# Second expert stage: gates spread through DRAM, all products in tiles of 64 by 64, two banks of sums

## The reference, cut to what matters

```python
flat = _rmsnorm(x, ln2_w).reshape(-1, Cx)
probs = jax.nn.softmax(flat @ router_w.T, axis=-1)
tp, ti = jax.lax.top_k(probs, TOPK)
tp = tp / (jnp.sum(tp, axis=-1, keepdims=True) + 1e-09)
weights = jnp.sum(tp[..., None] * jax.nn.one_hot(ti, NE, dtype=flat.dtype), axis=1)
for e in range(NE):
    hh = jax.nn.silu(flat @ w1[e].T) * (flat @ w3[e].T)
    out = out + weights[:, e:e + 1] * (hh @ w2[e].T)
return x + out.reshape(Bx, Tx, Cx)
```

## Time and profile before

| | us |
|---|---|
| median of 3 runs | 2643.34 |
| lowest and highest | 2638.82 and 2643.75 |
| the profiled execution's own time | 2647.51 |
| its span in the trace | 2645.6 |
| the second expert stage in it, from the first transpose | 2283.96 to 2645.6 |

### The profile page before, as it was taken

One profiled execution on the slowest core, in us unless ns is written; L12 is line 12 of the kernel. 1 busy time (PEld: TensorE's weight loads), 2 busy tenths in 40 slices (PEclk: granted clock), 3 DMA queues, 4 the chain that ended last, 5 costly groups with the idle time before them and its releaser, 6 DMA issues.

```text
span 2645.6 us, 50217 instructions
## 1 busy us (share of the span) xinstructions
PE 2413.0 (91%) x17762; PEld 1076.1 (41%) x17762; DVE 1835.3 (69%) x4773; ACT 1414.1 (53%) x2468; POOL 424.6 (16%) x505
## 2 busy tenths in 40 slices
PE   8987779999999999998699998987799998799999
PEld 3326623333333333334344444565544444433333
DVE  4566679888888888882456656569676773366665
ACT  2116727777777777774254453427567665144343
POOL 2002200000000000004322322132000012310110
PEclk9996769999999999997699996656699998599999
DMA  2114511010111101023555551245522242500110
GB/s 93 24 30 130 198 49 38 26 38 26 36 28 29 35 26 38 26 54 81 140 134 138 133 156 39 59 117 181 195 65 65 66 103 58 122 17 17 33 25 12
DMA packets 247843, 190.43 MB, mean 72 GB/s; under 512 B 190299, under 2 KB 195580, under 8 KB 247340
## 3 DMA queue, kind: packets, MB, share of 16 engines
q1 hardware_dynamic: 234426, 158.95, 22.4%
q0 software_dynamic: 10368, 19.06, 2.5%
q10 hardware_dynamic: 2808, 9.22, 1.5%
HBM read 121.58 MB, written 65.63 MB: 71 GB/s over the span
## 4 chain that ended last, share of the span: by engine, by line
PE 77%; DVE 8%; ACT 4%; DMA 3%; issue 3%; POOL 2%; SPq 1%; DVEq 0%; ACTq 0%; POOLq 0%
PE ps L1580 10%; PE ps L1486 7%; PE ps L1551 6%; PE ps L2785 4%; PE ps L2797 4%; PE ps L2291 4%; PE ps L2773 4%; PE ps L2306 4%; PE ps L1191 3%; PE ps L1165 3%; PE ps L364 3%; PE ps L1576 2%; PE ps L376 2%; PE ps L1103 2%; DMA mo_gate<-wg_d 1%
## 5 line engine op out<-in xcount | busy, mean ns | idle before, releaser
L1666 DVE TENSOR_REDUCE att_mpart<-ps 128x1 f32<-128x512 f32 x1024 | 633.5, 682 | 55.7 <-PE ps L1486 50.6
L1624 ACT ACTIVATE att_p<-ps 128x704 f32<-128x704 f32 x768 | 546.7, 761 | 214.8 <-PE ps L1551 207.6
L1580 PE MATMUL ps<-att_p,att_v 128*9 128x352 f32 x3072 | 300.7, 462 | 0.1
L1486 PE MATMUL ps<-att_kT,att_qT 64*128 64x512 bf16 x1024 | 281.0, 386 | 21.0 <-DMA att_qz<-qt_d 8.4
L1551 PE MATMUL ps<-att_qT,att_kT 64*128 64x352 bf16 x1536 | 251.4, 317 | 7.3 <-ACT att_p L1624 6.9
L1280 DVE TENSOR_REDUCE cau_mpart<-ps 128x1 f32<-128x512 f32 (+5 forms) x384 | 193.0, 551 | 81.2 <-PE ps L1106 61.1
L1247 ACT ACTIVATE cau_p<-ps 128x704 f32<-128x704 f32 (+6 forms) x272 | 171.5, 661 | 82.4 <-PE ps L1165 49.8
L2365 ACT ACTIVATE mo_g<-ps 128x768 f32<-128x768 f32 x176 | 133.3, 809 | 139.6 <-PE ps L2291 139.6
L2859 ACT ACTIVATE mo_act<-ps 128x1024 f32<-128x1024 f32 (+1 forms) x108 | 102.8, 952 | 196.3 <-PE ps L2773 196.1
L1457 POOL DMA_DIRECT2D o_d<-att_o x128 | 64.1, 507 | 841.1 <-ACT att_o L1607 840.9
L1551 PEld LDWEIGHTS ps<-att_qT,att_kT 64*128 64x128 bf16 x1536 | 82.0, 93 | 273.0 <-issue 263.3
(11 more groups left out here) (417 smaller groups left out, 3933.0 us busy)
## 6 DMA issues: line engine op xcount, KB each, us to landing
mo_gate<-wg_d SPq DMA_DIRECT2D x176, 192.0 KB, 4.2
qt_d<-pre_qT SPq DMA_DIRECT2D x8, 1056.0 KB, 4.3
kt_d<-pre_kT SPq DMA_DIRECT2D x8, 1056.0 KB, 7.0
att_kT<-kt_d SPq DMA_DIRECT2D x32, 264.0 KB, 2.7
att_qT<-qt_d SPq DMA_DIRECT2D x32, 264.0 KB, 3.0
cqt_d<-cpr_qT SPq DMA_DIRECT2D x8, 1056.0 KB
cau_qT<-cqt_d SPq DMA_DIRECT2D x16, 528.0 KB, 4.1
o_d<-att_o POOLq DMA_DIRECT2D x128, 37.1 KB, 2.7
```

Source lines behind the costliest of these rows:

```text
L1486: mm = pe.matmul(ps[:, bank, :], qT[half(s), u, j * P:(j + 1) * P], kT[half(s), u, c * BANK:(c + 1) * BANK], start=True, stop=not near)
L1580: mm = pe.matmul(ps[32 * cg:32 * cg + DV, 7, 0:TH], v[:, u, i, s, :], p[:, r, s, :], start=i < 2, stop=i == FULL - 1)
L1624: e = act.activation(p[:, n % PRING, :, :], ps[:, bank:bank + 2, 0:TH], ACT.Exp)
L1666: red = dve.tensor_reduce(mpart[:, j, s, c:c + 1], ps[:, bank, :], AX.X, ALU.max)
```

## The change

The gates are no longer spread by products. `w_turn` turns the fp32 weights of a block as they are, ScalarE copies them to wT, `gates_out` writes 16 rows to DRAM, and `gates_in` reads them back, broadcast over 64 partitions, two DMAs for each pair of experts; `gated` multiplies both experts of a pair in one instruction of 1024 elements. `sone`, `sel`, `stk` and `parts_` go. The gates' chain is moved four steps ahead. `first`, `third` and `second` all use four products in tiles of 64 by 64. `second` sums the upper and the lower 64 hidden rows in two banks; ScalarE copies the one (`sums`) and VectorE adds the other (`whole`). SiLU is made by halves s, from three banks in turn.

```diff
-    Z1, Z3, SIDE, ACC = (0, 2), 4, 6, 7
-    ACT_RING, G_RING, GX = 3, 2, 4
-    place = {"t0": -13, "t0_cp": -10, "logits": -10, "top": -9, "gap": -8, "exp": -6, "pick": -7, "prob": -6, "share": -5,
-             "parts": -4, "w_turn": -4, "w_turn_cp": -1, "stats": -15, "sums": 14, "y_turn": 17, "add": 18}
-    gate_step = [3 * (e // 2) - 3 + e % 2 for e in range(E)]
-    FIRST, LAST = -16, N_UNITS + 7
+    Z1_RING, Z3, SIDE, ACC = 3, 4, 6, (3, 7)
+    ACT_RING, G_RING, GATES = 3, 2, 4
+    QUADS = ((0, 0), (1, 1), (0, 1), (1, 0))
+    place = {"t0": -17, "t0_cp": -14, "logits": -14, "top": -13, "gap": -12, "exp": -10, "pick": -11, "prob": -10, "share": -9,
+             "w_turn": -8, "w_turn_cp": -5, "w_out": -5, "stats": -19, "sums": 14, "whole": 12, "y_turn": 17, "add": 18}
+    FIRST, LAST = -20, N_UNITS + 7
...
-        wT = nm.sb("wT", [P, 2, EN], BF16)
-        gx = nm.sb("gx", [P, GX, EN])
+        wT = nm.sb("wT", [2 * E, 2, EN])
+        gate = nm.sb("gate", [P, GATES, 2, EN])
+        gx = nm.sb("gx", [P, 2, 2, EN])
+        y0 = nm.sb("y0", [P, EN])
...
-                sp.dma_start(sone[s * C:s * C + E3, :], sel_d).then_inc(S["gate_in"], 16)
...
+            def gates_out(j):
+                sp.wait_ge(S["side_read"], use_no["w_turn", j] + 1)
+                at_least(sp, S["gx_made"], (j - 1) * EP)
+                sp.dma_start(wg_d[j % 2, 0:2 * E, 0:en(j)], wT[:, j % 2, 0:en(j)]).then_inc(S["w_out"], 16)
+            def gates_in(m):
+                j, q = divmod(m, EP)
+                sp.wait_ge(S["w_out"], 16 * (j + 1))
+                at_least(sp, S["gx_made"], m - GATES + 1)
+                for s in range(2):
+                    src = wg_d[j % 2, s * E + 2 * q:s * E + 2 * q + 2, 0:en(j)]
+                    sp.dma_start(gate[halves(s), m % GATES, :, 0:en(j)],
+                                 src.rearrange("(o e) n -> o e n", o=1).broadcast_to([C, 2, en(j)])).then_inc(gate_sem[m % GATES], 16)
+            end_rows(0)
+            for step in range(FIRST, LAST):
+                j = at(step, place["w_out"])
+                if j is not None:
+                    gates_out(j)
+                m, rest = divmod(step + 5, 3)
+                if rest == 0 and 0 <= m < MK * EP:
+                    gates_in(m)
...
+                j = at(step, 7)
+                if j is not None and j > 0:
+                    end_rows(j)
                     store(j - 1)
...
             norm(0)
-            pool.wait_ge(S["gate_in"], 16 * 4)
...
+            norm(1)
             for j in range(MK):
-                if j + 1 < MK:
-                    norm(j + 1)
+                if j + 2 < MK:
+                    norm(j + 2)
                 rests(j)
...
-            def gates(j, e):
-                side_free(e, j)
-                for s in range(2):
-                    mm = pe.matmul(ps[halves(s), SIDE, 0:en(j)], sel[s * C:s * C + E3, e * C:(e + 1) * C],
-                                   wT[s * C:s * C + E3, j % 2, 0:en(j)], start=True, stop=True)
...
-                at_least(pe, S["act_made"], n - 1)
                 for s in range(2):
-                    mm = pe.matmul(ps[:, Z1[n % 2] + s, 0:en(j)], w13[halves(s), 0, column(n):column(n) + P],
-                                   x1[halves(s), j % 2, 0:en(j)], start=True, stop=True)
-                mm.then_inc(S["z1_mm"], 1)
+                    at_least(pe, S["act_made"], 2 * n + s - Z1_RING + 1)
+                    for c in range(2):
+                        mm = pe.matmul(ps[halves(c), (2 * n + s) % Z1_RING, 0:en(j)],
+                                       w13[halves(s), 0, column(n) + c * C:column(n) + (c + 1) * C],
+                                       x1[halves(s), j % 2, 0:en(j)], start=True, stop=True)
+                    mm.then_inc(S["z1_mm"], 1)
...
+                for s, c in QUADS:
+                    e = experts[c % len(experts)]
+                    mm = pe.matmul(ps[halves(c), Z3 + s, 0:en(j)], w13[halves(s), 1, column(n) + c * C:column(n) + (c + 1) * C],
+                                   gx[halves(s), m % 2, e % 2, 0:en(j)], start=True, stop=True)
...
-                for s in range(2):
-                    mm = pe.matmul(ps[halves(s), ACC, 0:en(j)], w2[:, column(n) // P, :], g[:, n % G_RING, s, 0:en(j)],
-                                   start=i == 0, stop=i == UN - 1)
+                for r, s in QUADS:
+                    mm = pe.matmul(ps[halves(s), ACC[r], 0:en(j)], w2[halves(r), column(n) // P, :],
+                                   g[halves(r), n % G_RING, s, 0:en(j)], start=i == 0, stop=i == UN - 1)
...
-                act.activation(y[:, 0:en(j)], ps[:, ACC, 0:en(j)], ACT.Identity).then_inc(S["y_cp"], 1)
+                at_least(act, S["y_cp"], j)
+                act.activation(y0[:, 0:en(j)], ps[:, ACC[0], 0:en(j)], ACT.Identity).then_inc(S["y0_cp"], 1)
...
-                    act.activation(act1[:, n % ACT_RING, :, 0:w], ps[:, Z1[n % 2]:Z1[n % 2] + 2, 0:w], ACT.Silu)\
-                        .then_inc(S["act_made"], 1)
+                    for s in range(2):
+                        act.wait_ge(S["z1_mm"], 2 * n + s + 1)
+                        act.activation(act1[:, n % ACT_RING, s, 0:w], ps[:, (2 * n + s) % Z1_RING, 0:w], ACT.Silu)\
+                            .then_inc(S["act_made"], 1)
...
+            def gated(m):
+                j, q = divmod(m, EP)
+                dve.wait_ge(gate_sem[m % GATES], 32 * (m // GATES + 1))
+                if q == 0:
+                    dve.wait_ge(S["side_read"], use_no["t0", j] + 1)
+                at_least(dve, S["z3_mm"], 3 * (m - 2) + 3)
+                dve.tensor_tensor(gx[:, m % 2, :, 0:en(j)], x1[:, j % 2, 0:en(j)].unsqueeze(1).broadcast_to([P, 2, en(j)]),
+                                  gate[:, m % GATES, :, 0:en(j)], ALU.mult).then_inc(S["gx_made"], 1)
+            def whole(j):
+                dve.wait_ge(S["y0_cp"], j + 1)
+                if j > 0:
+                    dve.wait_ge(S["side_mm"], use_no["y_turn", j - 1] + 1)
+                dve.tensor_tensor(y[:, 0:en(j)], ps[:, ACC[1], 0:en(j)], y0[:, 0:en(j)], ALU.add).then_inc(S["y_cp"], 1)
...
-                for e in range(E):
-                    j = at(n, gate_step[e] + 1)
-                    if j is not None:
-                        gated(j, e)
+                m, rest = divmod(n + 2, 3)
+                if rest == 0 and 0 <= m < MK * EP:
+                    gated(m)
...
+        wg1_d = dram("wg1_d", [2, 2 * 8, BANK])
```

More of the change, by code:

```diff
@@ L2530, in expert_units @@
         w2 = nm.sb("w2", [P, UN, C])
-        sel = nm.sb("sel", [P, E * C], BF16)
-        sone = nm.sb("sone", [P, E * C])
         iota = nm.sb("iota", [P, E])
@@ L2656, in store @@
                     sp.dma_start(rows_of(h_out, j, s), tiles_of(res[:, :, :], j, s)).then_inc(S["stored"], 16)
-            for j in range(MK):
-                end_rows(j)
-                if j + 2 < MK:
-                    sp.wait_ge(S["xn_made"], j + 1)
-                    load(sp, j + 2, j % 2)
-                if j > 0:
+            def gates_out(j):
[18 more added lines that the diff above has]
+                    gates_in(m)
+                j = at(step, -18 - UN)
+                if j is not None and j >= 2:
+                    sp.wait_ge(S["xn_made"], j - 1)
+                    load(sp, j, j % 2)
+                j = at(step, 7)
+                if j is not None and j > 0:
+                    end_rows(j)
                     store(j - 1)
@@ L2780, in third @@
                 at_least(pe, S["g_made"], n)
-                pe.wait_ge(S["side_read"], use_no[experts[-1], j] + 1)
-                m = P // len(experts)
-                for i, e in enumerate(experts):
-                    for s in range(2):
-                        mm = pe.matmul(ps[i * m:(i + 1) * m, Z3 + s, 0:en(j)],
-                                       w13[halves(s), 1, column(n) + i * m:column(n) + (i + 1) * m],
-                                       gx[halves(s), e % GX, 0:en(j)], start=True, stop=True)
+                m = j * EP + experts[0] // 2
+                pe.wait_ge(S["gx_made"], m + 1)
+                for s, c in QUADS:
+                    e = experts[c % len(experts)]
+                    mm = pe.matmul(ps[halves(c), Z3 + s, 0:en(j)], w13[halves(s), 1, column(n) + c * C:column(n) + (c + 1) * C],
+                                   gx[halves(s), m % 2, e % 2, 0:en(j)], start=True, stop=True)
                 mm.then_inc(S["z3_mm"], 1)
@@ L2803, in _ @@
             for step in range(FIRST, LAST):
-                if step == -13:
-                    pe.wait_ge(S["gate_in"], 16 * 4)
+                if step == place["logits"]:
+                    pe.wait_ge(S["gate_in"], 16 * 2)
                 if step == -3:
                     pe.wait_ge(S["w_in"], 16 * 4)
-                    pe.wait_ge(S["sel_made"], 2)
                 if step == 0:
@@ L2817, in _ @@
                 side_parts(step, parts)
-                for e in range(E):
```

(13 more changed lines are left out.)

64 lines of the change are left out of this document (21 added, 43 removed).

## The result

The changed kernel takes **2603.64 us** (median of 4 runs, 2602.29 to 2606.85) against 2641.08 (2638.11 to 2643.75) before: ratio 0.986, 95% interval 0.9846 to 0.9875. Forecast were 2615 and a range of 2588 to 2636. The profiled execution took 2603.57, its span is 2601.8, and TensorE's mean granted clock 0.906.

The account below looks back on a forecast made before the run. TensorE was taken as the bound, busy for all 40.92 us of a block. Terms -53.8 + 22.5 + 3 + 1 - 1.4 = -28.7, applied to the median of 2643.3, gave 2615 us, range 2588 to 2636.

Parts of the forecast that it names:

- TensorE, -53.8: TensorE's blocks: one tile shape and no gates' products make a block 34.2 instead of 40.9, 53.8 us less in eight.
- Rival (3): TensorE's 64 by 64 passes: weights not loaded ahead, each pass loses 0.05, 30.5 in all, giving 2645; chance 0.07.
- The stall, +22.5: Block starts: copy of sums queued behind exp delays `whole` and TensorE, 21.7 over blocks 1 to 7, plus 0.8 in block 0.
- 3.1 late: Start of blocks 1 to 7: `third` of unit 3 starts at 10.8 instead of 7.7, 3.1 us lost for good.
- the 3 named: Sign of being right: TensorE waits for VectorE 3 us a block at the start of seven blocks.
- The 0.8 of block 0: Block 0, without a copy of sums: the exp alone delays a SiLU half by 0.8 us.
- VectorE and GpSimd, +3: Gating from two SBUF operands is slowed beside GpSimd's work: 0 to 0.8 a block, 0.4 taken, +3 in eight.
- The start, +1: Stage start: weights ready earlier, then gates through DRAM, fewer SiLU banks and slow clock; bounds -2 and +5, +1 taken.
- The end, -1.4: Twelve small units get faster while `whole` joins the last chain: between -2.3 and +0.5, -1.4 taken.
- (1) No stall: Block starts: exp and sums don't meet as said, or the table load hides; 2592, chance 0.13.
- (2) Gates late: Gates through DRAM: gating waits for them 2.4 us once a block, 19 in eight; 2634, chance 0.15.
- (4) Halves of `first` one after the other: Split `first`: second half's products start only after the first half's, 0.86 more each, 82 in all; 2677, chance 0.08.

Follow-up runs that it names:

- run 2: Changed kernel with the softmax's exp replaced by a plain copy on ScalarE, so no table loads (gates not the reference's): 2595.6 us, ratio 0.9816.
- run 8: Changed kernel with the copy of sums ahead on ScalarE, gates from one tanh instead of exp, and pick one unit later: 2587.7 us, ratio 0.9805.
- run 1: Changed kernel with the copy of the sums put ahead of the next block's exp in ScalarE's queue: 2594.6 us, ratio 0.9826.
- 4: Changed kernel with the gates' chain begun earlier (third buffer for x1) and gates from one tanh instead of exp: 2601.3 us, ratio 0.9837.
- 10: Changed kernel with only the norm's row sums moved earlier, so GpSimd's norm runs beside the first gating: 2619.6 us, ratio 0.9936.
- 7: Changed kernel with two banks instead of three for the products that SiLU reads: 2608.6 us, ratio 0.9882.
- 9: Changed kernel with `first` alone back in products of 64 by 128, still by halves into three banks: 2637.3 us, ratio 0.9988.
- 11: Changed kernel with the copy of sums ahead of the exp on ScalarE and pick one unit later, exp kept: 2596.4 us, ratio 0.9851.
- 12: The changed kernel itself measured once more, nothing altered: 2605.4 us, ratio 0.9887.

## Why the prediction was right, step by step

- **TensorE, -53.8: right.** Passes stay at 0.43 in 64 by 64, shown in the rows above, and a block without its stall is 34.2. Rival (3) was set against the Trainium skill (TensorE: Matmul & The Clock Gate, Part 3, The mechanism), which lets weight loads overlap only where the row group differs; by that rule a `first` behind a `third` would not be 0.86. The trace speaks against it in this shape too: `first`'s weights are loaded at 2420.16 while `third`, of the same rows, runs to 2420.77.
- **The stall, +22.5: mechanism right, size off.** Counted from `third` of unit 0 (2437.78): SiLU ends at 3.1 (3.2 forecast; its two halves take 1.08, not 1.20), copy at 5.2 (5.4; it starts 0.16 after the exp's start, in the exp's time), `whole` at 5.9 (6.2), `third` of unit 2 starts at 7.1 (7.4), g of unit 2 at 8.9 (9.5, the small operations of pick overlap), `third` of unit 3 at 10.2 (10.8). The step that failed is "3.1 late": it is 2.5, which is 4.2 over seven blocks. `whole` waits 1.55, not 1.8. TensorE's recorded waits there, 1.53 and 0.32, are less than the 3 named and than the 2.6 lost; recorded ends of products lie late, so a wait shows shorter than it is. The 0.8 of block 0 came as some 0.9, but not by the path given: block 0 takes 34.3 where its dense time is about 33.4, since no `y_turn` falls into it (its unit 6 takes 2.58, later blocks' 3.32). Some 0.3 is lost before g of unit 1 and 0.6 before g of unit 2, which waits for gating and pick on VectorE. The 0.6 is there without an exp too (3.13 between the two g, in run 2 as well) and goes when pick stands later (2.56 in run 8). So at most 0.3 is the exp's, and the size was luck. That the queue's order makes more than half of the stall in the other blocks is shown by run 1 (1.36 of 2.6). Of the rest run 8 takes another 0.76, and 0.4 stays.
- **VectorE and GpSimd, +3: the lower bound came.** Of the 36 gatings one took 1.67, near the start, and none else over 1.23. GpSimd's work lies elsewhere in the block, so the term of 3 stood for nothing in this order. The mechanism is real (runs 4 and 10), but whether it pays hangs on one position in the order, and the trace of before could tell that only for before.
- **The start, +1: +1.0 in this pair, by luck: two errors cancel.** The weights were ready 2.7 earlier (2.8 forecast), and DRAM took 6.4 from the write's issue at 2283.49 to the gating at 2289.90 (5.8 forecast). The step that failed is `third` of unit 0: forecast 0.6 earlier than before, it starts 2.0 later (23.0 after the part before, against 21.0). The gating is through at 2291.13, but `third` starts at 2293.17. TensorE's order puts the second block's transpose, `first` and the second block's logits ahead of it, which the forecast had as done already, and that transpose waits for GpSimd's norm:

```profile
2286.80 1.12 PE L2747 MATMUL ps<-eye,mo_xn 128*128 128x128 f32 x4 [3.96 <-POOL mo_xn L2715]
...
2293.17 1.09 PE L2797 MATMUL ps<-mo_gx,mo_w 64*64 64x512 f32 x8
```

  TensorE's clock gives 1.0 back: g comes 1.23 after this `third`, against 2.20 before, where the clock was still 1.2 GHz. In windows of the changed kernel and of run 1 the third column from the end is the granted clock, 0.50 for 1.2 GHz and 1.00 for 2.4:

```profile
2290.00:2292.00 2.00, 2.00 (x8) 0.29 (x4) 1.13 (x1) 1.38 (x3) 0.00 (x0) 0.53 0.98 238
2292.00:2294.00 2.00, 2.00 (x18) 1.33 (x20) 0.69 (x8) 0.77 (x2) 0.00 (x0) 1.00 1.04 238
```

```profile
2293.00:2295.00 2.00, 2.00 (x10) 1.68 (x8) 0.00 (x0) 0.67 (x2) 0.00 (x0) 0.50 1.02 234
2299.00:2301.00 2.00, 2.00 (x16) 0.60 (x12) 0.86 (x12) 1.98 (x3) 0.00 (x0) 0.74 0.00 0
```

  The changed kernel went from 1.2 to 2.4 GHz at about 2292, 22 after the part before, run 1 only at about 2300, 29 after it (2271.4). In both TensorE had been busy without a gap ahead of the rise, from 2286.80 and from 2287.71. In run 1 `third` of unit 0 still ran at 1.2 GHz, and the first g came at 25.9 instead of 24.2. Over the runs that leave the start's order as it is (after, 1, 2, 7, 9, 11, 12) the first g comes 23.8 to 26.4 after the part before, so this term is known to some 3 us only.
- **The end, -1.4: -0.7.** The small units gave 1.0 (14.25 to 13.22), the last chain took 0.4 back.
- **The sum.** The stage gave 35.4 where 28.7 was put, 6.7 more: 4.2 that the stall didn't cost, 3 that the port didn't, less 0.7 that the end didn't give, and 0.2 left over. Of the 11.4 between 2615 and 2603.6 that is 6.7; 2.3 is the median of before, which was 2643.3 when the forecast was made and is 2641.1 in the comparison; the last 2.4 (0.4 of it rounding) is less than the part ahead of the stage moves.
- **The rivals.** (1) No stall: refuted by `whole`'s waits, 11.7 in blocks 1 to 7, and by run 1. (2) Gates late: in the whole stage gating waits for its DMA once, 7.34 at the start. (3) Refuted, as above. (4) Halves of `first` one after the other: refuted by 0.86 a group.
